# Second attention of a fused layer: order of the row maxima, two transposes of them per step, and the causal mask moved to VectorE

## The chip, the cores and the metric

One core of a Trainium2 chip (trn2) runs the whole layer in one launch. The time is that of the device for one execution, in microseconds (us); lower is better.

## The reference, cut to what matters

The layer is a first attention (16 heads of 64), a second attention (16 query heads and 4 key heads of 16, with a rotary encoding) and a mixture of 8 experts, over 4 batches of 1024 rows of 256. Only the second attention changes:

```python
# q: [4, 1024, 16, 16], k and v: [4, 1024, 4, 16] repeated for 4 query heads each
scores = jnp.einsum('bqhd,bkhd->bhqk', q, k) * scale
causal = jnp.tril(jnp.ones((S, S), dtype=bool))
scores = jnp.where(causal[None, None], scores, jnp.finfo(scores.dtype).min)
probs = jax.nn.softmax(scores, axis=-1)
attn = jnp.einsum('bhqk,bkhd->bqhd', probs, v).reshape(B, S, NH * HD)
```

## The kernel before, in words

`attention_two` goes through 16 steps, one for each batch and key head, and in each it treats four query heads. It is a software pipeline of three generations: in one step the engines prepare generation n1 (queries, keys, row maxima), compute scores, exponentials and most outputs of generation n2, and finish the last outputs of n3. The first step has only n1 and the last ones have no n1; the fourteen between run in a loop of two steps per turn. `step` of each engine is a written order over 48 slots k, one for each entry of `UNITS2`: a unit is a half c of the queries (512 columns) and a tile j of 128 keys, and it has one slot for each of the four heads. Twelve units: c=0 has j=0..3 with 512, 384, 256 and 128 columns left by the causal cut, c=1 has four of 512 and then 512, 384, 256, 128.

In each slot TensorE computes one score tile [128 keys, up to 512 queries] into one of two PSUM banks `SC` (L1252), ScalarE takes its exponential into a ring of 16 tiles `b_P` (L1175), and GpSimd cuts the diagonal ones (L1122). At the last head of a unit TensorE multiplies the four tiles of the unit two before it with the values into `b_O` (L1266); this is 8 instructions in a row.

The exponential needs the row maximum of every query first. It is subtracted inside the score product: the query operand has 96 rows of split values and two more rows, a high part `hi` and a low part `lo` of the negated maximum, against two rows of ones in the keys. The maxima come from a product of its own, [128 queries, up to 512 keys], into one of three banks `MX` (L1303), which VectorE reduces along the row (L1219). There are 48 of these a step (`MAX2`): for each head, query tile i=0..7 and key half. 32 of them hold the diagonal; there TensorE adds a mask of 128 columns with a second matmul (L1306). `FILL2` spreads the 48 over slots 4 to 38, so that some slots have two. At slot 39 VectorE takes the larger of the two halves, negates (L1225), and at slot 40 TensorE turns the 32 columns (4 heads by 8 tiles) with one transpose (L1336); VectorE makes `hi` (L1232) and `lo` (L1234), and two DMAs write them into the query operand (L1152), for the scores of the next step.

One PSUM bank, `SM`, serves four things in turn, each of which waits until the one before it has been read: the five "stacks" (slots 0, 2, 8, 17, 26: eight transposes of loaded tiles, L1293, copied by ScalarE to the keys `b_K` and the four heads' queries `b_Q`, L1184), the transpose of the maxima, and the transposes of the outputs ("turn out", slots 13 and 31, L1278), from which VectorE makes the rows `A` two slots later (L1205, L1207). SyncE loads the values and the nine pieces of the next stack, and then the two rows of the maxima, in that order in its queue.

`normalise` is the first stage of the layer and `combine` the last; the change touches only their semaphores.

Of the kernel before, what the change touches and what calls it, by code (L numbers as in the profile page):

```python
# [16 lines left out]
P = 128  # L17
# [29 lines left out]
def normalise(nc, x, hold):  # L47

    with ExitStack() as ctx:
        sb = lambda name, shape, dt=F32: ctx.enter_context(nc.sbuf_tensor(name, shape, dt))  # L50
        sem = lambda name: ctx.enter_context(nc.semaphore(name))
# [990 lines left out]
MAX2 = [(h, i, c) for h in range(GROUP) for i, c in MAXU]  # L1042
# [3 lines left out]
STACK_SLOTS = (0, 2, 8, 17, 26)  # L1046
SCORE_BANKS, MAX_BANKS = 2, 3
TURN_SLOT, OUT_SLOTS = NU2 - 8, (16 + LAG2 + 5, LAG2 + 3)
FILL2 = {k: [] for k in range(NU2)}
for _n, _k in enumerate(STACK_SLOTS):  # L1050
    FILL2[_k].append(("stack", _n))
for _n in range(NU2):
    FILL2[4 + _n * (TURN_SLOT - 5) // NU2].append(("max", _n))


def attention_two(nc, stack_dram, V2, A2):

    with ExitStack() as ctx:
# [7 lines left out]
        Q = [sb(f"b_Q{i}", [STACK + 2, GROUP, S], BF16) for i in range(2)]  # L1066
# [5 lines left out]
        minus = sb("b_minus", [P, GROUP * ST_N])  # L1072
        hi = sb("b_hi", [GROUP * ST_N, P], BF16)
        lo = sb("b_lo", [GROUP * ST_N, P], BF16)
        ident = sb("b_ident", [P, P])
        identb = sb("b_identb", [P, P], BF16)
        maskb = sb("b_maskb", [P, P], BF16)
# [7 lines left out]
                 "turn_ready", "turn_copied", "minus_in", "scores_ready", "exp_done", "masked", "pv_done",  # L1085
                 "OT_copied", "OT_ready", "inv_ready", "A2_done", "v_in", "due")
        s = {k: sem(f"b_{k}") for k in names}
        loaded = [sem(f"b_loaded{i}") for i in range(2)]
        block = ctx.enter_context(nc.Block())
# [13 lines left out]
        def _(pool):  # L1103
            for m in (ident, identb, maskb):
                pool.memset(m[:, :], 0.0).then_inc(s["consts"], 1)
# [4 lines left out]
            pool.affine_select(out=maskb[:, :], in_=maskb[:, :], compare_op=ALU.is_ge, fill=NEG, base=0,  # L1110
# [18 lines left out]
        def _(sp):  # L1129
# [8 lines left out]

            def step(n1, n2, n3, p):
                if n1 is not None:  # L1140
# [9 lines left out]
                    sp.wait_ge(s["turn_copied"], n1 * 2 + 3)  # L1150
                    for n, part in enumerate((hi, lo)):
                        sp.dma_start(Q[p][STACK + n:STACK + n + 1, :, :].rearrange("p h s -> p (h s)"), part[:, :]).then_inc(s["minus_in"], 16)  # L1152

# [4 lines left out]
        def _(act):  # L1158
# [10 lines left out]
            def step(n1, n2, n3, p):  # L1169
                for k, (c, j, h) in enumerate(UNITS2):  # L1170
# [8 lines left out]
                    if n1 is not None:  # L1179
                        for what, n in FILL2[k]:  # L1180
                            if what == "stack":
                                act.wait_ge(s["stack_ready"], n1 * (GROUP + 1) + n + 1)
# [56 lines left out]
        def _(pe):  # L1239
# [29 lines left out]
            def turn_out(n, c, turned, stacks):  # L1269
# [4 lines left out]
                if stacks is not None:  # L1274
                    pe.wait_ge(s["stack_copied"], stacks + 1)
# [686 lines left out]
```

## Time and profile before

| what | value |
|---|---|
| median of 3 runs | 3100.15 us (3084.71 to 3101.48) |
| profiled execution, its own time | 3102.33 us |
| its span, first to last instruction | 3100.0 us |
| mean granted clock of TensorE | 0.912 of full |
| second attention in it | 1664 to 2335 us |
| busy in the whole span | PE 81%, DVE 51%, ACT 48%, POOL 28% |

PE is TensorE (PEld its weight loads), DVE VectorE, ACT ScalarE, POOL GpSimd, SPq the DMA queue of SyncE. A busy matmul is shown until its modelled end, so that matmuls issued back to back overlap in the record: the issue time of one is read from the distance of two starts. "Idle before" is the time for which an engine had nothing running, and what ended it stands behind the arrow; "issue" means that nothing in the profile ended it. A line "x2" merges two instructions.

### The profile page before, as it was taken

What the parts mean: (1) busy time and instruction counts of PE and PEld (TensorE: products, weight loads), DVE (VectorE), ACT (ScalarE), POOL (GpSimd) and SP (SyncE); (2) the same over time, 40 slices, a digit from 0 to 9 for tenths busy, and PEclk for the clock granted to TensorE, in tenths of its full rate; (3) what the DMA queues carried; (4) which work ended last, traced back from release to release, by engine and by line L of the source; (5) the groups of instructions that cost most, each with busy time, mean ns of one, the idle gap of its engine ahead of it and who ended that gap; (6) DMA issues with size and microseconds to landing.
All of it is one profiled execution on the core that took longest, in us unless ns stands there. A gap on an engine that the chain in (4) does not pass through costs nothing. (4 is left out here: it accounts for less than half of the span.)

```text
span 3100.0 us, 56250 instructions
## 1 busy us (share of the span) xinstructions
PE 2526.3 (81%) x12770; PEld 1441.6 (47%) x12771; DVE 1577.3 (51%) x3757; ACT 1475.8 (48%) x3174; POOL 882.8 (28%) x1636
## 2 busy tenths in 40 slices
PE   5999998999999999999465989888886509999950
PEld 3555565555655556554332333333334505666630
DVE  6666645666366663665476666666643302222225
ACT  3555544555355553555264666666664202222212
POOL 0244423444243442445132222222221160000035
PEclk7999999999999999999787999999999559999975
DMA  2001100101000010001233011111105422111124
GB/s 96 11 25 24 38 22 17 25 24 36 17 22 24 19 36 22 17 25 29 68 127 118 17 30 30 30 30 30 30 15 180 179 97 92 46 44 46 46 63 124
DMA packets 155681, 152.47 MB, mean 49 GB/s; under 512 B 67328, under 2 KB 127744, under 8 KB 153856
## 3 DMA queue, kind: packets, MB, share of 16 engines
q1 hardware_dynamic: 139008, 124.51, 13.0%
q0 software_dynamic: 6144, 16.79, 1.6%
q10 hardware_dynamic: 10368, 9.44, 0.9%
q8 instruction: 50, 0.82, 0.1%
q14 instruction: 111, 0.91, 0.1%
HBM read 87.76 MB, written 47.45 MB: 44 GB/s over the span
## 5 line engine op out<-in xcount | busy, mean ns | idle before, releaser
L1219 DVE TENSOR_REDUCE b_peak<-b_MX 128x1 f32<-128x512 f32 (+3 forms) x768 | 379.2, 551 | 206.4 <-PE b_MX L1306 181.6
L1175 ACT ACTIVATE b_P<-b_SC 128x512 f32<-128x512 f32 (+3 forms) x768 | 350.5, 490 | 206.2 <-PE b_SC L1252 185.5
L291 POOL TENSOR_TENSOR a_A<-a_A,a_P 128x512 f32<-128x512 f32 (+3 forms) x320 | 318.0, 994 | 308.8 <-PE a_O L595 296.1
L443 ACT ACTIVATE a_P<-a_SC 128x512 f32<-128x512 f32 (+3 forms) x640 | 293.7, 469 | 234.3 <-PE a_SC L578 200.7
L501 DVE CUSTOM_DVE_ANT_0 a_MX<-a_MX,a_causal 128x128 f32<-128x128 f32 (+3 forms) x512 | 249.9, 501 | 265.4 <-PE a_MX L641 258.0
L577 PE MATMUL a_SC<-a_QR,a_KR 128*128 128x512 f32 (+3 forms) x768 | 320.1, 421 | 15.1 <-DMA a_QS<-a_minusT 11.6
L641 PE MATMUL a_MX<-a_KR,a_QR 128*128 128x512 f32 (+3 forms) x768 | 290.0, 386 | 10.4 <-DVE a_peak L501 6.2
L1122 POOL TENSOR_SCALAR_AFFINE_SELECT b_P<-b_P 128x128 f32<-128x128 f32 x512 | 147.2, 292 | 525.5 <-ACT b_P L1175 520.5
L1252 PE MATMUL b_SC<-b_Q,b_K 98*128 98x512 bf16 (+3 forms) x768 | 250.4, 339 | 33.7 <-ACT b_P L1175 31.5
L578 PE MATMUL a_SC<-a_QS,a_KS 65*128 65x512 f32 (+3 forms) x768 | 268.4, 353 | 0.0
L1722 PE MATMUL e_GU<-W,e_hT 128*128 x576 | 260.9, 596 | 1.0 <-ACT e_hT L1774 0.8
L1303 PE MATMUL b_MX<-b_K,b_Q 96*128 96x512 bf16 (+3 forms) x768 | 238.3, 340 | 17.7 <-DVE b_peak L1219 12.0
L595 PE MATMUL a_O<-a_P,a_V 128*64 128x512 f32 (+3 forms) x1280 | 234.7, 479 | 17.3 <-POOL a_P L330 14.9
L577 PEld LDWEIGHTS a_SC<-a_QR,a_KR 128*128 128x128 f32 x768 | 148.7, 194 | 183.9 <-issue 112.1
L504 DVE TENSOR_REDUCE a_peak<-a_MX 128x1 f32<-128x512 f32 x256 | 169.7, 684 | 100.1 <-PE a_MX L641 100.0
L330 POOL TENSOR_SCALAR_AFFINE_SELECT a_P<-a_P 128x128 f32<-128x128 f32 x448 | 145.7, 334 | 233.8 <-ACT a_P L443 229.5
L291 DVE TENSOR_TENSOR a_A<-a_A,a_P 128x512 f32<-128x512 f32 (+3 forms) x320 | 199.3, 623 | 22.9 <-PE a_O L595 10.2
L618 PE MATMUL a_PK<-hold,a_W 128*128 (+1 forms) x384 | 188.7, 615 | 16.2 <-DMA a_W<-in_w_pair 6.9
L1835 POOL DMA_INDIRECT c_E<-done_rows,place x64 | 70.2, 1096 | 453.9 <-PEq L1820 434.7
L1812 DVE TENSOR_TENSOR e_gate<-e_gate,e_GU 128x512 f32<-128x512 f32 x72 | 49.5, 688 | 291.4 <-PE e_GU L1722 291.4
L641 PEld LDWEIGHTS a_MX<-a_KR,a_QR 128*128 128x128 f32 x768 | 147.5, 192 | 69.5 <-DVE a_peak L501 33.5
L443 ACT ACTIVATE a_A<-a_SC 128x512 f32<-128x512 f32 x128 | 76.6, 599 | 210.0 <-PE a_SC L578 209.3
(240 smaller groups left out, 4162.3 us busy)
## 6 DMA issues: line engine op xcount, KB each, us to landing
a_inv<-inv_rows SPq DMA_DIRECT2D x128, 128.0 KB, 3.0
stack_rows<-p_stk SPq DMA_DIRECT2D x32, 480.0 KB, 2.6
a_W<-in_w_pair SPq DMA_DIRECT2D x34, 384.0 KB, 3.5
b_stk<-stack_rows SPq DMA_DIRECT2D x136, 96.0 KB, 2.0
e_G<-sorted_rows SPq DMA_DIRECT2D x74, 128.0 KB, 2.0
sorted_rows<-r_zeros SPq DMA_DIRECT2D x6, 1536.0 KB, 5.9
done_rows<-e_out ACTq DMA_DIRECT2D x72, 128.0 KB, 1.7
W<-in_w SPq DMA_DIRECT2D x8, 1024.0 KB, 11.7
```

The source lines that it names most:

```text
L291: eng.tensor_tensor(acc[h][c][:, a:], acc[h][c][:, a:], buffer(n, h)[:, a:], ALU.add).then_inc(added[h], 1)
L443: act.activation(buffer(n, h)[:, a:], SC[h][:, a:], ACT.Exp, scale=DH1 ** -0.5).then_inc(s["exp_done"], 1)
L501: dve.tensor_tensor_reduce(MX[c % MAX_BANKS1][:, 0:w], MX[c % MAX_BANKS1][:, 0:w], causal[:, BANK - w:], 1.0, 3 * NEG, ALU.add, ALU.max, p ...
L577: pe.matmul(SC[h][:, a:], KR[p][h][:, keys], QR[p][h][:, queries], start=True, stop=False)
L578: pe.matmul(SC[h][:, a:], KS[p][h][:, keys], QS[p][h][:, queries], start=False, stop=True).then_inc(s["scores_ready"], 1)
L595: pe.matmul(O[DH1 * h:DH1 * (h + 1), a:], V[p][h][:, j, :], buffer(n, h)[:, a:], start=(j == 0), stop=(n in LAST)).then_inc(s["pv_done"], 1)
L641: pe.matmul(bank[:, 0:w], QR[p][h][:, i * P:(i + 1) * P], KR[p][h][:, ch * BANK:ch * BANK + w], start=True, stop=True).then_inc(s["max_rea ...
L1175: act.activation(probs[k % RING2][:, a:], SC[k % SCORE_BANKS][:, a:], ACT.Exp, scale=DH2 ** -0.5).then_inc(s["exp_done"], 1)
L1219: dve.tensor_reduce(peak[:, h, i, ch:ch + 1], MX[n % MAX_BANKS][:, 0:w], AX.X, ALU.max).then_inc(s["max_used"], 1)
L1252: pe.matmul(SC[k % SCORE_BANKS][:, a:], K[p2][:, j * P:(j + 1) * P], Q[p2][:, h, c * BANK + a:(c + 1) * BANK], start=True, stop=True).then ...
L1303: last = pe.matmul(MX[n % MAX_BANKS][:, 0:w], Q[p][0:STACK, h, i * P:(i + 1) * P], K[p][0:STACK, ch * BANK:ch * BANK + w], start=True, sto ...
L1722: last = pe.matmul(GU[i][half][:, :], hT[i][:, kt, :], W13[:, bass.ds(e, 1), kt, half * FFN:(half + 1) * FFN].rearrange("p a f -> p (a f)" ...
```

## The change

- **Order and place of the maxima.** `MAX2` now goes by halves: first the 16 of query tiles 0 to 3 (all heads), then the 32 of tiles 4 to 7. Maximum u is placed in slot u + 5, one in every slot; the last five (43 to 47) fall into slots 0 to 4 of the next step, beside that step's first scores.
- **Two transposes.** `minus`, `hi` and `lo` exist once for each half. The first half's is turned at slot 23 of its own step, the second's at slot 6 of the next step. SyncE sends the second pair of rows at the head of its step, before the value and stack loads, and the first pair behind them. Scores of the second half wait for their rows at slot 16.
- **Stacks** at slots 0, 2, 7, 11, 15 instead of 0, 2, 8, 17, 26; the query operand is laid out by half and then head, so that ScalarE's copy writes two pieces of 512.
- **Mask.** TensorE's 32 mask matmuls are gone. VectorE reduces the 32 diagonal tiles with one instruction that adds a mask tile `causal` and takes the maximum (`tensor_tensor_reduce`, the form that the first attention uses at L501); the other 16 are reduced as before.
- **Semaphores.** `normalise`'s are kept until after `attention_two`, cleared there by GpSimd, and four of their numbers are used for `combine`'s `fetched`.

```diff
-MAX2 = [(h, i, c) for h in range(GROUP) for i, c in MAXU]
+MAX2 = [(h, i, c) for first in (True, False) for h in range(GROUP) for i, c in MAXU if (i < BANK // P) == first]
-STACK_SLOTS = (0, 2, 8, 17, 26)
+STACK_SLOTS = (0, 2, 7, 11, 15)
+MAX_START = 5
+HALF_MAX = (16, NU2)
+TURN_SLOTS = (MAX_START + 18, MAX_START + NU2 + 1 - NU2)
-TURN_SLOT, OUT_SLOTS = NU2 - 8, (16 + LAG2 + 5, LAG2 + 3)
-    FILL2[4 + _n * (TURN_SLOT - 5) // NU2].append(("max", _n))
+OUT_SLOTS = (16 + LAG2 + 5, LAG2 + 3)
+MAX_AT = {k: [n for n in range(NU2) if n + MAX_START == k] for k in range(MAX_START + NU2)}
...
 SyncE
+            def minus_rows(n, p, c):
+                sp.wait_ge(s["turn_copied"], n * 4 + 2 * c + 3)
+                for m, part in enumerate((hi[c], lo[c])):
+                    sp.dma_start(Q[p][STACK + m:STACK + m + 1, c, :, :]..., part[:, :]).then_inc(minus_in[c], 16)
+                if n2 is not None:
+                    minus_rows(n2, 1 - p, 1)
                 if n1 is not None:
...
                     load((n1 + 1) % STEPS2, 1 - p)
+                    minus_rows(n1, p, 0)
...
 VectorE
+            def reduce_max(n, u):
+                h, i, ch = MAX2[u]
+                w = min(BANK, (i + 1) * P - ch * BANK)
+                dve.wait_ge(s["max_ready"], n * NU2 + u + 1)
+                if ch == i * P // BANK:
+                    dve.sem_inc(s["due"], 1)
+                    dve.tensor_tensor_reduce(MX[u % MAX_BANKS][:, 0:w], MX[u % MAX_BANKS][:, 0:w], causal[:, BANK - w:], 1.0, 3 * NEG,
+                                             ALU.add, ALU.max, peak[:, h, i, ch:ch + 1]).then_inc(s["max_used"], 1)
+                else:
+                    dve.tensor_reduce(peak[:, h, i, ch:ch + 1], MX[u % MAX_BANKS][:, 0:w], AX.X, ALU.max).then_inc(s["max_used"], 1)
+                for c in range(2):
+                    if u == HALF_MAX[c] - 1:
+                        dve.wait_ge(s["max_used"], n * NU2 + u + 1 + MAX_BANKS)
+                        dve.tensor_reduce(minus[c][:, :, :], peak[:, :, 4 * c:4 * c + 4, :], AX.X, ALU.max,
+                                          negate=True).then_inc(s["minus_ready"], 1)
+            def turn(n, c):
+                dve.wait_ge(s["turn_ready"], n * 2 + c + 1)
+                dve.wait_ge(minus_in[c], n * 32 + 1)
+                dve.tensor_copy(hi[c][:, :], T).then_inc(s["turn_copied"], 1)
+                dve.wait_ge(s["turn_copied"], n * 4 + 2 * c + 2)
+                dve.tensor_tensor(lo[c][:, :], T, hi[c][:, :], ALU.subtract).then_inc(s["turn_copied"], 1)
...
 TensorE
-                    if diag:
-                        last = pe.matmul(MX[n % MAX_BANKS][:, w - P:w], identb[:, :], maskb[:, :], start=False, stop=True)
+                if k == 16 * c:
+                    pe.wait_ge(minus_in[c], n2 * 32 + 33)
+            def turn_minus(n, c):
+                pe.wait_ge(s["minus_ready"], n * 2 + c + 1)
+                pe.transpose(SM[0:GROUP * ST_N // 2, 0:P], ...).then_inc(s["turn_ready"], 1)
+                    if n1 is not None and k in STACK_SLOTS:
+                        n = STACK_SLOTS.index(k)
+                        if n == 0:      # loaded; rows_done(n3, 0)
...
+                        elif n == 2 and n2 is not None:
+                            turned(n2, 1)        # hi and lo of the second half read SM
+                        elif n == 4 and n3 is not None:
+                            rows_done(n3, 1)     # rows A of turn out, slot 13
+                        else:
+                            stacked(n1, n)       # ScalarE's copy before
+                        stack(n1, p, n)
+                    if n2 is not None and k == TURN_SLOTS[1]:
+                        stacked(n1, 2) ...
+                        turn_minus(n2, 1)
+                    if n1 is not None and k == TURN_SLOTS[0]:
+                        stacked(n1, 5)
+                        turn_minus(n1, 0)
...
 layer
+        nc.clear_and_free_semaphores(sems)
+        fetched = [nc.alloc_semaphore(name=f"c_fetched{i}", num=m.num) for i, m in enumerate(sems)][0:4]
```

The comments in the TensorE part of this cut are added here for the reader.

## Rows read from the trace of the kernel before

**Rows 1.** Windows over one full step: engines' busy us (instructions), granted clock, DMA.
```profile
...
2102.00:2142.70 40.70, 35.50 (x273) 15.05 (x273) 25.47 (x55) 27.12 (x56) 9.24 (x32) 1.00 0.11 29
...
```

**Rows 2.** Timeline of ScalarE: start, us, operation, idle before it.
```profile
...
1698.48 1.01 ACT L1184 ACTIVATE b_K<-b_SM 96x1024 bf16<-96x1024 bf16 x1
...
2142.24 0.60 ACT L1175 ACTIVATE b_P<-b_SC 128x512 f32<-128x512 f32 x1 [2.56 <-issue]
...
2263.28 1.01 ACT L1184 ACTIVATE b_K<-b_SM 96x1024 bf16<-96x1024 bf16 x1
...
```

**Rows 3.** Groups by shape, second attention: count, busy us, mean ns, idle before.
```profile
...
L1219 DVE TENSOR_REDUCE b_peak<-b_MX 128x1 f32<-128x512 f32 x384 | 254.7, 685 | 53.7 <-PE b_MX L1306 30.9 <-PE b_MX L1303 22.7
...
L1122 POOL TENSOR_SCALAR_AFFINE_SELECT b_P<-b_P 128x128 f32<-128x128 f32 x512 | 147.2, 292 | 525.5 <-ACT b_P L1175 520.5 <-issue 0.4
...
L1184 ACT ACTIVATE b_Q<-b_SM 96x1024 bf16<-96x1024 bf16 x64 | 65.5, 1024 | 24.9 <-PE b_SM L1293 24.8
...
```

**Rows 4.** Timeline of TensorE over one full step.
```profile
...
2100.53 0.65 PE L1293 MATMUL b_SM<-b_identb,b_stk 128*96 128x128 bf16 x8
2101.01 0.60 PE L1252 MATMUL b_SC<-b_Q,b_K 98*128 98x512 bf16 x2
...
2113.83 0.39 PE L1252 MATMUL b_SC<-b_Q,b_K 98*128 98x512 bf16 x1
...
2115.47 0.65 PE L1293 MATMUL b_SM<-b_identb,b_stk 128*96 128x128 bf16 x8 [0.91 <-DVE A L1207]
...
2135.93 0.28 PE L1336 MATMUL b_SM<-b_ident,b_minus 128*32 128x128 f32 x1 [0.26 <-DVE b_minus L1225]
...
2139.26 0.85 PE L1266 MATMUL b_O<-b_P,b_V 128*32 128x384 f32 x8
2140.05 0.64 PE L1293 MATMUL b_SM<-b_identb,b_stk 128*96 128x128 bf16 x8
...
```

**Rows 5.** Timeline of TensorE in the last step, without stacks and maxima.
```profile
...
2323.08 0.60 PE L1252 MATMUL b_SC<-b_Q,b_K 98*128 98x512 bf16 x2
2324.14 0.88 PE L1252 MATMUL b_SC<-b_Q,b_K 98*128 98x512 bf16 x2 [0.47 <-ACT b_P L1175]
2324.95 1.07 PE L1266 MATMUL b_O<-b_P,b_V 128*32 128x512 f32 x8
2325.95 0.50 PE L1252 MATMUL b_SC<-b_Q,b_K 98*128 98x384 bf16 x2
...
2328.52 0.39 PE L1252 MATMUL b_SC<-b_Q,b_K 98*128 98x256 bf16 x2
...
2330.76 0.29 PE L1252 MATMUL b_SC<-b_Q,b_K 98*128 98x128 bf16 x2
...
```

**Rows 6.** Timeline of VectorE in the step of rows 4.
```profile
...
2114.99 0.42 DVE L1207 TENSOR_TENSOR A<-b_SM,b_inv 128x256 f32 x1 [0.47 <-DVE b_inv L1205]
...
2136.68 0.28 DVE L1234 TENSOR_TENSOR b_lo<-b_SM,b_hi 32x128 bf16<-32x128 f32 x1
```

**Rows 7.** Groups by shape, VectorE in the first attention.
```profile
...
L501 DVE CUSTOM_DVE_ANT_0 a_MX<-a_MX,a_causal 128x512 f32<-128x512 f32 x128 | 88.7, 693 | 2.6
...
L501 DVE DVE_READ_ACCUMULATOR2_ANT a_peak<- 128x1 f32 x512 | 69.6, 136 | 2.7 <-issue 1.9
...
```

**Rows 8.** Timeline of VectorE in the first attention.
```profile
...
1417.46 0.69 DVE L501 CUSTOM_DVE_ANT_0 a_MX<-a_MX,a_causal 128x512 f32<-128x512 f32 x1
...
1418.07 0.33 DVE L501 CUSTOM_DVE_ANT_0 a_MX<-a_MX,a_causal 128x128 f32<-128x128 f32 x1
...
```

**Rows 9.** Timeline of TensorE from the first step into the second.
```profile
...
1694.93 1.06 PE L1293 MATMUL b_SM<-b_identb,b_stk 128*96 128x128 bf16 x8 [0.77 <-DVE b_lo L1234]
1697.35 1.04 PE L1252 MATMUL b_SC<-b_Q,b_K 98*128 98x512 bf16 x2 [1.36 <-DMA b_Q<-b_lo]
...
```

**Rows 10.** Windows of TensorE alone: busy us, granted clock.
```profile
...
1982.00:1984.00 2.00, 1.90 (x10) 0.50 0.00 0
...
2318.00:2321.00 3.00, 2.74 (x12) 0.50 0.00 0
...
```

More of the change, by code:

```diff
@@ new lines, in stacked, with turned, rows_done, stack @@
+            def stacked(n, count):
+                pe.wait_ge(s["stack_copied"], n * (GROUP + 1) + count + 1)
+            def turned(n, c):
+                pe.wait_ge(s["turn_copied"], n * 4 + 2 * c + 3)
+            def rows_done(n, c):
+                pe.wait_ge(s["A2_done"], n * 2 + c + 2)
+            def stack(n1, p, n):
+                for t in range(ST_N):
+                    last = pe.transpose(TR[:, t * P:(t + 1) * P], stk[p][:, t, (n - 1) % (GROUP + 1), :], identb[:, :])
+                last.then_inc(s["stack_ready"], 1)
@@ new lines, in maximum @@
+            def maximum(n, p, u):
+                h, i, ch = MAX2[u]
+                w = min(BANK, (i + 1) * P - ch * BANK)
+                if (i, ch) == MAXU[0]:
+                    stacked(n, h + 2)
+                pe.wait_ge(s["max_used"], n * NU2 + u + 1)
+                last = pe.matmul(MX[u % MAX_BANKS][:, 0:w], Q[p][0:STACK, i // 4, h, i % 4 * P:(i % 4 + 1) * P],
+                                 K[p][0:STACK, ch * BANK:ch * BANK + w], start=True, stop=True)
+                last.then_inc(s["max_ready"], 1)
@@ L1316, in step @@
                         output(n3, p, NU + unit)
-                    if n1 is not None:
-                        for f in FILL2[k]:
-                            fill(n1, n3, p, *f)
-                    if n2 is not None:
-                        if k == 0:
-                            scores(n2, 1 - p, 0)
-                        if last_head and unit >= 0:
-                            output(n2, 1 - p, unit)
-                        if k == OUT_SLOTS[0]:
-                            turn_out(n2, 0, n2 + 1, None if n1 is None else (n1 + 1) * (GROUP + 1))
@@ new lines, in step @@
+                    for u in MAX_AT[k]:
+                        if n1 is not None:
+                            maximum(n1, p, u)
+                    for u in MAX_AT.get(k + NU2, ()):
+                        if n2 is not None:
+                            maximum(n2, 1 - p, u)
+                    if n2 is not None and k == 0:
+                        scores(n2, 1 - p, 0)
+                    if n2 is not None and last_head and unit >= 0:
+                        output(n2, 1 - p, unit)
+                    if n2 is not None and k == TURN_SLOTS[1]:
+                        if n1 is not None:
+                            stacked(n1, 2)
+                        else:
+                            rows_done(n3, 0)
+                        turn_minus(n2, 1)
```

145 lines of the change are left out of this document (61 added, 84 removed).

## The prediction

> **What bounds the kernel now.** I read the page's slices first: the second attention lies between 1664 and 2335 us, and no engine is full in it. The chain that ended last covers only the tail of the layer, so the stage has to be read by its own rhythm. Two starts of ScalarE's key copy give the step: from 1698.48 to 2263.28 are 14 intervals, 40.34 us each [rows 2]. The windows over one step show TensorE with 35.5 busy us of 40.7, ScalarE 27.1, VectorE 25.5, GpSimd 9.2 [rows 1]; TensorE's busy time includes the modelled tails, so it is less occupied than it seems.
>
> The timeline of one step tells more [rows 4]. From stack to stack it takes 2140.05 - 2100.53 = 39.52 us; slots 0 to 15 take 13.30 of them (to 2113.83) and slots 16 to 47 take 26.22. Most other steps are about 1.1 us longer, because ScalarE comes late to its first exponential with nothing that the profile can name (2.56 us of "issue") [rows 2]. I take this as untouched by the change.
>
> The last step has no stacks and no maxima, and shows the bare rhythm of scores [rows 5]. A unit of four 512-wide tiles starts at 2323.08. Two scores are issued, 0.22 us apart (0.60 for two against 0.39 for one). The third waits for an exponential until +1.06, the output block starts at +1.87 and lasts 1.00, and the next unit starts at +2.87. So a unit is two score banks refilled at ScalarE's pace, plus what TensorE does after its last score, which ScalarE can't fill. The same rows give 2.57 for a unit of 384, 2.24 for 256 and 1.71 for 128 (2330.76, then at +0.93 an output block of 384, which takes 2140.05 - 2139.26 = 0.79 [rows 4]). Each 128 columns less in the output block save 0.21. A maximum between two scores hides in those waits; one after the fourth score does not. That is the bound: TensorE's written order, against ScalarE through two banks; VectorE comes in only where two maxima share a slot.
>
> **The change part by part.**
>
> *Slots 16 to 47.* Removed here are two stacks, the stop at slot 17 (TensorE waits 0.91 us for VectorE's rows [rows 4]), the transpose at slot 40 with its 0.26 us wait [rows 4], and the density of 1.37 maxima a slot with a mask on two of three. What is left is the bare rhythm plus one maximum after the fourth score, 0.06 to 0.22 us (0.22 for 512 columns, in proportion below). By unit: unit 4 has an output block of 256 columns, 2.87 - 0.42 + 0.17 = 2.62; unit 5 one of 128, 2.87 - 0.63 + 0.22, with the new transpose at slot 23 about 0.2, so 2.65; unit 6 3.08; unit 7 3.08 + 0.49 for turn out = 3.57 (four transposes of 128 columns, as long here as the eight of a stack, 2101.01 - 2100.53 = 0.48 [rows 4]); unit 8 3.15, as VectorE makes rows in it; units 9 to 11 2.72, 2.45 and 2.1. Sum 22.3, against 26.2: a gain of 3.9 us.
>
> *Slots 0 to 15.* Here all five stacks, one transpose of maxima and a turn out go through the one bank. I follow the order from the first stack's issue at 0, with durations from the rows. A copy takes ScalarE about 0.92 (1.02 recorded [rows 3], less the overlap of its end), and about 1.9 lie between a stack's issue and its copy's release. The second stack comes at 2.6, as now. The four new maxima put slot 4 at 4.3 (now 3.94). Slot 6 turns the second half at 5.9. The stack at slot 7 must wait until `lo` is made; from such a transpose to the end of `lo` are 2136.68 + 0.28 - 2135.93 = 1.03 us [rows 4, 6], so it starts at 7.1 and TensorE, there at 6.2, idles 0.9. Slot 8 begins at 8.1. The first maximum of the second head waits for this stack's copy until 8.9. Slot 11's stack goes at 9.7, the unit ends at 11.4. Turn out at slot 13 waits for ScalarE, which does the copy of slot 11 and then that of the outputs, until 12.1, and ends at 12.55. The stack at slot 15 has to wait for VectorE's rows: it still has the maximum of slot 14 to finish (13.3), then 1.09 for reciprocal and product (0.25, 0.42 idle-and-start, 0.42 [rows 6]), so 14.45, where TensorE has been since 12.85: 1.6 us idle against 0.9 now. Slot 16 starts at 15.9, against 13.3: a loss of 2.6 us.
>
> *Net:* -1.3 us a step, over 15 steps -19.5.
>
> *Masks.* The 32 mask matmuls are 0.06 us of issue each (a quarter of 0.22), 1.9 us a step; that gain is inside the unit prices, not beside them. VectorE takes them over. The first attention has the same instruction: 693 ns for 512 columns [rows 7] against 685 for the plain reduction [rows 3], and a read of the accumulator, 136 ns [rows 7]. The read overlaps nearly all of itself: the next instruction starts 0.61 us after the 512-wide one [rows 8]. So one costs 0.01 to 0.15 us more; I take 0.04, by the start-to-start distance, 1.3 us a step. The cover is VectorE's idle time, 15 us of 40.7 [rows 1]; above the value taken, up to 3.5 us a step would lie on VectorE, and by units it is full only in 9 to 11 (2.1 us of reductions in 2.1 to 2.7), so at most 1 us a step comes through.
>
> *First step and last.* The first loses its turn at the end: now a stack starts at 1694.93 and the first scores at 1697.35, 1.36 of it on the DMA of `lo` [rows 9]; the second step's scores will find their rows long there. That gives 2; filling only 43 maxima instead of 48 gives 2.7 on VectorE, less some 1.2 for maxima that wait for the closer stacks. The last step gains five maxima and a transpose, +1. Together -2.5.
>
> *DMAs and queues.* Each step issues four row DMAs for two, all on SyncE. The pair at the head of its step now stands before the value load and nine stack loads, whose data are needed a step later: nothing. The pair's own data take 1697.35 - 1694.9 = 2.5 us from `lo` [rows 9]; made at 7.0, they are there at 9.5, and slot 16 comes at 15.9. GpSimd's masks (292 ns each [rows 3]) don't change. Clearing the semaphores is one short work of GpSimd between two stages, taken as nothing; bound 1 us. The split copy writes as many elements: 1.02.
>
> *Sum.* The profiled execution has 3102.3 (span 3100.0); with -19.5 - 2.5 = -22 it is 3080. It lies 2 us above the median shown, so the median to come is 3078.
>
> **The rivals.**
>
> *The stalls of slots 7 and 15 cost nothing.* If ScalarE, which has three copies more in these slots, is itself the limit there, only the relief counts: -3.9 x 15 - 2.5 = -61, 3039. For it: slots 0 to 3 are ScalarE's already. Against: ScalarE has run dry by then in my walk, 0.9 us before slot 7's copy and 1.7 before slot 15's. Chance 0.15.
>
> *The one bank gets the upper hand (slower).* Seven users in 16 slots hand it on, each after the reader of the one before. If a hand-over costs 0.45 us more than walked at each of them, slots 0 to 15 take 19 us, the step is 1.8 longer, and the time is 3100 + 27 - 2.5 = 3125. It decides from 17.2 us for these slots. For it: the wait at slot 17 was 0.9 us even with four slots between turn out and stack, and VectorE may be behind. Against: VectorE has fewer maxima there. Chance 0.13.
>
> *The clock.* TensorE's clock fell to 1.2 GHz (0.50) for stretches at 1982 and 2318 [rows 10], after idle pieces at a step's head and in the thin last step. The new slots 8 to 15 have much idle time. If the clock fell there in every step, its 5 us of work would take 3 more for part of it: net +1.7 x 15, 3123. The Trainium skill ("TensorE: Matmul & The Clock Gate", Part 4: PE-mode transpose) says that the full clock does not engage for transposes, and the change crowds six groups of them into these slots; no row here parts transposes from other work, and by that rule the rival's sum would hold. Chance 0.1.
>
> *VectorE binds.* The reduction with the mask costs its full 0.15: +1 us a step, 3093. Rows 8 speak against it. Chance 0.12.
>
> **How the numbers follow.** The forecast itself has 0.5, with 3060 to 3096 as its own range (a step's net between 2.5 less and 0.1 less). About 0.5% (15 us) is what a measurement of this kernel tells from no change. Faster than 3084.6: 0.35 of my own case, 0.15 of the first rival and 0.04 of the last: 0.54. Slower than 3115.6: the second and third rival in most of their width, 0.17. Within: 0.29. Range 3040 to 3116: it takes in the first rival's value and stops short of the slow ones.
>
> **What would show it.** In the timeline of TensorE after: slot 16 some 15.9 us after the first stack of its step; waits of about 0.9 us at the stack of slot 7 for `b_lo`, and 1.6 at slot 15 for `A`; 22.3 us from there to the next stack; no wait on the DMA of the second pair; VectorE without a long idle piece between steps; the key copy every 39.0 us. The prediction is wrong if slots 0 to 15 take over 17.2 us or under 14, if half clock shows in most steps, or if the masked reductions start over 0.7 us apart.

## The result and the profile after

The changed kernel takes 3103.88 us (median of 20 runs, 3097.41 to 3117.61) against 3098.56 us for the one before (20 runs, 3084.71 to 3103.41). The ratio is 1.0025, with a 95% interval of 1.0013 to 1.0036. The forecast was 3078 us, a gain of 22. The change costs about 5 us instead: within what I called no change, but on the other side of it.

The stage can be cut out of the trace, from its first stack to the end of the last rows `A`. Before, these are 1665.18 and 2335.39, so 670.2 us; after, 1663.59 and 2336.03, so 672.4. That is 2.2 us more where 22 less were forecast. What lies outside the stage was 2429.8 us before and 2426.3 after, and goes from 2416 to 2433 over the profiled executions of this study, though nothing in it is changed. So below I give the ratio of each kernel, and the stage time of its one profiled execution. For e2 and e7 that execution lies 8 and 6 us below the median of its kernel, so their stage times are less firm than the ratios.

From the changed kernel's page, the head and the slices of the clock:

```profile
span 3098.7 us, 56383 instructions
...
PE 2511.4 (81%) x12274; PEld 1415.4 (46%) x12275; DVE 1620.2 (52%) x4317; ACT 1475.0 (48%) x3174; POOL 883.5 (29%) x1636
...
PEclk8999999999999999999786999999999559999975
```

One step of it in windows, to be set beside [rows 1]:

```profile
2141.40:2182.30 40.90, 35.48 (x242) 14.19 (x242) 28.90 (x93) 27.16 (x57) 9.28 (x32) 0.96 0.11 28
```

TensorE has 31 instructions fewer (32 masks gone, one transpose more) and is as long busy. VectorE has 3.4 us more. ScalarE and GpSimd are as before. The step is not shorter, and the granted clock is 0.96, not 1.00.

ScalarE's key copies give the mean step [rows 2]. These are the second and the last of the 16:

```profile
1693.72 1.01 ACT L1194 ACTIVATE b_K<-b_SM 96x1024 bf16<-96x1024 bf16 x1
...
2264.19 1.01 ACT L1194 ACTIVATE b_K<-b_SM 96x1024 bf16<-96x1024 bf16 x1
```

(2264.19 - 1693.72) / 14 = 40.75 us, against 40.34. The forecast had 39.0. The first copy starts at 1664.71, so first to second takes 29.01, against 32.17.

TensorE through slots 0 to 16 of one step, to be set beside the first rows of [rows 4]:

```profile
1770.60 0.65 PE L1318 MATMUL b_SM<-b_identb,b_stk 128*96 128x128 bf16 x8
...
1773.27 0.65 PE L1318 MATMUL b_SM<-b_identb,b_stk 128*96 128x128 bf16 x8 [0.51 <-ACT b_K L1194]
...
1776.86 0.28 PE L1334 MATMUL b_SM<-b_ident,b_minus 128*16 128x128 f32 x1 [0.38 <-DVE b_minus L1240]
...
1778.23 0.65 PE L1318 MATMUL b_SM<-b_identb,b_stk 128*96 128x128 bf16 x8 [0.57 <-DVE b_lo L1250]
...
1780.08 0.23 PE L1328 MATMUL b_MX<-b_K,b_Q 96*128 96x128 bf16 x1 [0.60 <-ACT b_Q L1196]
...
1780.65 0.62 PE L1318 MATMUL b_SM<-b_identb,b_stk 128*96 128x128 bf16 x8
...
1782.87 0.66 PE L1304 MATMUL b_SM<-b_ident,b_OT 128*128 128x128 f32 x4
...
1785.46 0.87 PE L1318 MATMUL b_SM<-b_identb,b_stk 128*96 128x128 bf16 x8 [1.70 <-DVE A L1222]
...
1786.58 1.51 PE L1298 MATMUL b_O<-b_P,b_V 128*32 128x384 f32 x8
...
1788.02 0.61 PE L1284 MATMUL b_SC<-b_Q,b_K 98*128 98x512 bf16 x1
```

All the stalls that I walked through are there, each a little later: the stack of slot 7 at +7.63 (forecast 7.1), slot 11's at +10.05 (9.7), slot 15's at +14.86 (14.45) after 1.70 us of waiting (1.6). Slot 16 then comes at +17.42, not at 15.9: behind the wait the output block of 384 columns takes 1.51 us where it had taken 0.85 [rows 4], because the clock has fallen. Windows of TensorE in this kernel, the first just behind that wait and the second behind the wait for `b_lo` in another step:

```profile
1786.00:1788.00 2.00, 2.00 (x13) 0.50 0.45 111
...
2148.00:2150.00 2.00, 1.97 (x11) 0.50 0.03 4
```

A step in which the clock stays full has slot 16 at +16.5.

Slots 16 to 47 of a step, TensorE again; the first row and the rows at which units 5 to 11 and the next stack start:

```profile
2157.18 0.39 PE L1284 MATMUL b_SC<-b_Q,b_K 98*128 98x512 bf16 x1
...
2159.90 0.39 PE L1284 MATMUL b_SC<-b_Q,b_K 98*128 98x512 bf16 x1
...
2162.58 0.38 PE L1284 MATMUL b_SC<-b_Q,b_K 98*128 98x512 bf16 x1
...
2165.77 0.39 PE L1284 MATMUL b_SC<-b_Q,b_K 98*128 98x512 bf16 x1
...
2169.46 0.38 PE L1284 MATMUL b_SC<-b_Q,b_K 98*128 98x512 bf16 x1
...
2172.66 0.34 PE L1284 MATMUL b_SC<-b_Q,b_K 98*128 98x384 bf16 x1
...
2175.54 0.28 PE L1284 MATMUL b_SC<-b_Q,b_K 98*128 98x256 bf16 x1
...
2178.11 0.23 PE L1284 MATMUL b_SC<-b_Q,b_K 98*128 98x128 bf16 x1
...
2179.57 0.39 PE L1328 MATMUL b_MX<-b_K,b_Q 96*128 96x512 bf16 x1 [0.24 <-DVE b_peak L1233]
...
2180.67 0.65 PE L1318 MATMUL b_SM<-b_identb,b_stk 128*96 128x128 bf16 x8
```

The units are 2.72, 2.68, 3.19, 3.69, 3.20, 2.88, 2.57 and 2.56 us: 23.49 together. The forecast had 2.62, 2.65, 3.08, 3.57, 3.15, 2.72, 2.45 and 2.1: 22.3.

The masked reductions themselves cost what was forecast. By shape:

```profile
L1236 DVE TENSOR_REDUCE b_peak<-b_MX 128x1 f32<-128x512 f32 x256 | 175.8, 687 | 5.8 <-PE b_MX L1328 5.7
...
L1233 DVE CUSTOM_DVE_ANT_0 b_MX<-b_MX,b_causal 128x512 f32<-128x512 f32 x128 | 89.7, 701 | 54.6 <-PE b_MX L1328 52.8
...
L1233 DVE DVE_READ_ACCUMULATOR2_ANT b_peak<- 128x1 f32 x512 | 72.3, 141 | 0.0
```

From the start of a 512-wide one to the next instruction it is mostly 0.61 or 0.62 us, and 0.60 for a plain one.

### The profile page after: what moved, and what is told of

Read it like the earlier page. It is cut to its first block and busy times, and to the rows that moved or that the text cites. A ratio compares the mean times of both kernels' runs of the same rounds, so it can differ in the third digit from the quotient of the medians.

```text
span 3098.7 us, 56383 instructions
## 1 busy us (share of the span) xinstructions
PE 2511.4 (81%) x12274; PEld 1415.4 (46%) x12275; DVE 1620.2 (52%) x4317; ACT 1475.0 (48%) x3174; POOL 883.5 (29%) x1636
## 3 DMA queue, kind: packets, MB, share of 16 engines
q1 hardware_dynamic: 139520, 124.52, 12.9%
q14 instruction: 144, 1.18, 0.1%
## 5 line engine op out<-in xcount | busy, mean ns | idle before, releaser
L1233 DVE CUSTOM_DVE_ANT_0 b_MX<-b_MX,b_causal 128x128 f32<-128x128 f32 (+3 forms) x512 | 251.3, 500 | 180.0 <-PE b_MX L1328 161.0
L582 PE MATMUL a_SC<-a_QR,a_KR 128*128 128x512 f32 (+3 forms) x768 | 319.7, 420 | 14.4 <-DMA a_QS<-a_minusT 11.1
L1328 PE MATMUL b_MX<-b_K,b_Q 96*128 96x512 bf16 (+3 forms) x768 | 260.1, 349 | 12.0 <-DVE b_peak L1233 5.9
L1284 PEld LDWEIGHTS b_SC<-b_Q,b_K 98*128 98x128 bf16 x768 | 74.8, 99 | 235.2 <-ACT b_P L1186 191.9
L1236 DVE TENSOR_REDUCE b_peak<-b_MX 128x1 f32<-128x512 f32 x256 | 175.8, 687 | 5.8 <-PE b_MX L1328 5.7
```

What stands on the lines that cost most here:

```text
L582: pe.matmul(SC[h][:, a:], KR[p][h][:, keys], QR[p][h][:, queries], start=True, stop=False)
L1233: dve.tensor_tensor_reduce(MX[u % MAX_BANKS][:, 0:w], MX[u % MAX_BANKS][:, 0:w], causal[:, BANK - w:], 1.0, 3 * NEG, ALU.add, ALU.max, pea ...
L1284: pe.matmul(SC[k % SCORE_BANKS][:, a:], K[p2][:, j * P:(j + 1) * P], Q[p2][:, c, h, a:], start=True, stop=True).then_inc(s["scores_ready"], 1)
L1328: last = pe.matmul(MX[u % MAX_BANKS][:, 0:w], Q[p][0:STACK, i // 4, h, i % 4 * P:(i % 4 + 1) * P], K[p][0:STACK, ch * BANK:ch * BANK + w], ...
```

## The experiments

All were timed against the kernel before, in several rounds in which its own median was 3094.5 to 3098.6 us; so kernels of different rounds are compared by their ratios, not by their medians. A step is the mean interval of the key copies; the two parts are means over the 14 steps between first and last, from the first stack to slot 16 and from there to the next stack; "full clock" is the first part in steps without half clock and without a late start of ScalarE. Half clock is summed from windows of 2 us between 1704 and 2264.

| kernel | ratio (95%) | median us | stage | step | slots 0-15 (full clock) | slots 16-47 | half clock us |
|---|---|---|---|---|---|---|---|
| before | 1 | 3098.56 | 670.2 | 40.34 | 14.40 (13.3) | 26.09 | 18 |
| after | 1.0025 (1.0013-1.0036) | 3103.88 | 672.4 | 40.75 | 17.23 (16.5) | 23.56 | 34 |
| e1 | 1.0040 (1.0026-1.0054) | 3108.62 | 684.0 | 41.14 | 14.95 (13.5) | 26.33 | 34 |
| e2 | 0.9964 (0.9949-0.9980) | 3083.29 | 657.5 | 39.82 | 16.40 (16.1) | 23.47 | 10 |
| e3 | 0.9912 (0.9894-0.9929) | 3069.30 | 635.5 | 38.22 | 14.82 (14.4) | 23.44 | 5 |
| e4 | 0.9979 (0.9968-0.9991) | 3087.13 | 666.4 | 40.27 | 16.88 (16.6) | 23.44 | 0 |
| e5 | 0.9875 (0.9854-0.9895) | 3056.13 | 632.0 | 38.04 | 14.61 (14.3) | 23.48 | 3 |
| e6 | 1.0000 (0.9985-1.0015) | 3094.82 | 668.6 | 40.38 | 14.56 (13.3) | 25.97 | 24 |
| e7 | 0.9985 (0.9972-0.9997) | 3088.10 | 660.0 | 39.54 | 14.06 (13.1) | 25.63 | 10 |
| e8 | 0.9952 (0.9934-0.9970) | 3081.21 | 658.7 | 39.94 | 16.59 (15.9) | 23.40 | 17 |
| e9 | 0.9835 (0.9823-0.9848) | 3043.13 | 618.2 | 37.21 | 14.12 (13.3) | 23.14 | 17 |
| e10 | 0.9858 (0.9841-0.9875) | 3052.27 | 628.3 | 38.03 | 14.60 (14.2) | 23.48 | 7 |
| e11 | 0.9799 (0.9787-0.9812) | 3033.82 | 611.7 | 36.73 | 13.82 (12.9) | 22.95 | 14 |

### e1: the mask alone, on the kernel before

```diff
+                                if ch == i * P // BANK:
+                                    dve.tensor_tensor_reduce(MX[...][:, 0:w], MX[...][:, 0:w], causal[:, BANK - w:], 1.0, 3 * NEG,
+                                                             ALU.add, ALU.max, peak[:, h, i, ch:ch + 1])...
-                        last = pe.matmul(MX[n % MAX_BANKS][:, w - P:w], identb[:, :], maskb[:, :], start=False, stop=True)
```

> The kernel before with one part of the change alone: the causal mask of the 32 diagonal maxima is added by VectorE and TensorE's 32 mask matmuls a step are gone; order, stacks and transposes as before. Theory of the one bank (slots 0 to 15 lose because stacks, transposes and turn out share one PSUM bank): this part brings a gain, since the maxima weigh on TensorE's order and VectorE has room: the step falls by 0.5 to 1 us, 3084 to 3091. Rival, VectorE binds: between slots 4 and 38 VectorE already does 1.37 reductions a slot, so 0.04 us more for each of 32 lengthens the step by up to 1.3 us: 3110 to 3118.

Measured: 12 us slower (0.40%), stage +13.8. So this half of the change is a loss by itself. A step at full clock is 0.5 us longer (39.5 to 40.0), and half clock is on for 34 us instead of 18. In the old order 13 of the 35 slots with maxima hold two, and TensorE waits for a bank of them. Its weight loads for the maxima, in both kernels from 1704 to 2264, show what they waited for; first before, then e1:

```profile
L1303 PEld LDWEIGHTS b_MX<-b_K,b_Q 96*128 96x128 bf16 x667 | 65.1, 98 | 77.0 <-DVE b_peak L1219 51.2 <-issue 9.1
```

```profile
L1309 PEld LDWEIGHTS b_MX<-b_K,b_Q 96*128 96x128 bf16 x658 | 63.8, 99 | 102.1 <-DVE b_peak L1222 41.9 <-DVE b_peak L1225 36.1 <-issue 7.0
```

Waits for VectorE's reduction go from 51.2 us to 78.0: every reduction longer by little, each of them in front of a waiting product.

### e2: the order alone, with the mask on TensorE

```diff
-                if ch == i * P // BANK:
-                    dve.tensor_tensor_reduce(...)
+                if ch == i * P // BANK:
+                    last = pe.matmul(MX[u % MAX_BANKS][:, w - P:w], identb[:, :], maskb[:, :], start=False, stop=True)
```

> The changed kernel with the mask back on TensorE (32 matmuls of 128 columns a step, all 48 reductions plain): the order of the maxima, the two transposes and the closer stacks alone. Theory of the one bank: the loss is in these, and the mask's matmuls come back on top: 3106 to 3116. Rival, VectorE binds: with plain reductions the units at the end of the step (slots 44 to 47, 2.55 us where 2.1 were expected) shrink to 2.1 and the time falls under that of the changed kernel, 3094 to 3100.

Measured: 3083.29 us, under both numbers. The order alone is worth 0.36%, and the mask on VectorE takes it away again. The tile `b_SM` tells where, by TensorE's waits for it. After, from 1704 to 2264:

```profile
  DVE A L1222: 23.0, 13
  DVE b_lo L1250: 7.5, 13
  ACT b_K L1194: 6.7, 13
```

and e2, from 1704 to 2200:

```profile
  DVE A L1222: 18.0, 12
  ACT b_K L1194: 6.2, 12
  DVE b_lo L1245: 2.8, 10
```

The numbers are us and times: 1.77 us each for `A` against 1.50, 0.58 for `b_lo` against 0.28. Both waits end in a chain of VectorE that starts behind its reductions, so what the masked ones cost beyond plain ones comes through there, although VectorE idles for 12 of 40.9 us. That TensorE merely arrives later in e2, since it has the mask products to do, is ruled out by e8: without any mask the wait for `A` is 1.50 us as well (18.0 us in 12 waits). VectorE's timeline shows the chain of `A`. After, three masked reductions (512, 128 and 256 columns) and the reciprocal:

```profile
2153.08 0.70 DVE L1233 CUSTOM_DVE_ANT_0 b_MX<-b_MX,b_causal 128x512 f32<-128x512 f32 x1 [0.75 <-PE b_MX L1328]
...
2154.48 0.25 DVE L1220 RECIPROCAL b_inv<-b_SM 128x16 f32<-128x16 f32 x1
```

e2, the same three as plain ones, in one row:

```profile
2130.51 1.27 DVE L1231 TENSOR_REDUCE b_peak<-b_MX 128x1 f32<-128x512 f32 x3 [0.88 <-PE b_MX L1326]
2131.70 0.25 DVE L1220 RECIPROCAL b_inv<-b_SM 128x16 f32<-128x16 f32 x1
```

That is 1.40 us before the reciprocal against 1.19; in after it is 1.40 and 1.25 in turn from step to step, in e2 always 1.19. At full clock the waits make 0.4 us a step, and half clock shrinks from 34 to 10 us as well. The unit at the end, which the rival made VectorE's, falls from 2.55 us to 2.39, not to 2.1. Slots 16 to 47 don't show it (23.47), because units 4, 9 and 10, which have the mask products back, are 0.05 to 0.07 us longer each. So the rival was right in kind and had a third of its size.

### e3: turn out behind the last stack

```diff
-OUT_SLOTS = (16 + LAG2 + 5, LAG2 + 3)
+OUT_SLOTS = (16 + LAG2 + 5, 17)
...
-                        elif n == 4 and n3 is not None:
-                            rows_done(n3, 1)
...
                     if n1 is not None and k == TURN_SLOTS[0]:
-                        stacked(n1, 5)
+                        rows_done(n3, 1)
```

> The changed kernel with one move: the transposes of the last outputs (turn out of the second half) come at slot 17, behind the last stack, instead of slot 13, so that the stack at slot 15 no longer waits for VectorE's rows A. Theory of the one bank: the 1.7 to 1.8 us of idle TensorE at slot 15 go, and most of it is kept, 1.2 to 1.8 us a step: 3077 to 3086. Rival, the clock: if the loss is TensorE's half clock in slots 7 to 17 and that comes from the idle piece at slots 6 to 7, it stays, and 3094 to 3100 remain. Rival, the wait is covered because ScalarE is the limit there: 3100 to 3106.

Measured: 3069.30, better than both. The stage falls by 36.9 us against after, from 672.4 to 635.5. Slots 0 to 15 at full clock go from 16.5 to 14.4. In the timeline of TensorE of e3 the stack of slot 15 no longer waits, and turn out fits in behind it:

```profile
2122.32 0.65 PE L1318 MATMUL b_SM<-b_identb,b_stk 128*96 128x128 bf16 x8 [0.58 <-DVE b_lo L1250]
...
2127.54 0.64 PE L1318 MATMUL b_SM<-b_identb,b_stk 128*96 128x128 bf16 x8
...
2128.28 0.85 PE L1298 MATMUL b_O<-b_P,b_V 128*32 128x384 f32 x8
...
2129.78 0.60 PE L1304 MATMUL b_SM<-b_ident,b_OT 128*128 128x128 f32 x4
```

One wait, in one of seven turns of a bank, hid the gain of the whole reordering.

### e4: the idle pieces filled with products

```diff
                         elif n == 2 and n2 is not None:
+                            again(n1, p, 2, 4)
                             turned(n2, 1)
                         elif n == 4 and n3 is not None:
+                            again(n1, p, 10, 7)
                             rows_done(n3, 1)
```

`again` repeats a product of 512 columns into a bank of the maxima that VectorE has read: 4 and 7 extra ones a step, whose results nobody reads.

> The changed kernel with repeated products in its two idle pieces: 4 extra 512-column products before TensorE's wait at slot 7 and 7 before its wait at slot 15, into the bank of a maximum that is computed again behind them, so that nothing else changes. Theory of the clock: the granted clock stays at 1.00 through the step, where it now falls to 0.50 for some 4 us in most steps (0.96 over the step), and 0.7 to 1.3 us a step come back: 3085 to 3093. Theory of the one bank alone: the clock may stay up, but the waits stand and the half clock lay beside them: 3100 to 3106.

Measured: 3087.13. Half clock is gone from all 14 steps, though TensorE does 11 products more. The step shortens by 0.48 us and the stage by 6.0. The median fell by 17, but by the two intervals that is 14 with 5 to either side, so the stage is the better price: half clock costs this kernel 6 us or somewhat more, and slots 0 to 15 keep their 16.6. The waits are the larger part.

### e5: mask on TensorE and turn out later

The edits of e2 and e3 together.

> The order and the two transposes of the change, the mask on TensorE as before, and the turn out of the second half at slot 17 behind the last stack (the two runs that were faster than the changed kernel, put together). Theory of two independent losses (the bank's chain at slot 15, and VectorE's masked reduction): they add, slots 0 to 15 fall from 16.1 to about 14.0 us, the step to 37.7 us, and the time to 3060 to 3068. Rival, both losses are one and the same wait (a masked reduction only matters because it delays VectorE's rows A): then removing the wait already got all, and this equals the run with the later turn out, 3067 to 3074, or is slower by the mask's matmuls.

Measured: 3056.13, stage 632.0. The mask's return is worth only 3.5 us of the stage once the wait for `A` is gone; 15 in the presence of that wait (672.4 to 657.5). That fits e2: most of its cost went through `A`. The medians of e3 and e5 lie 13 us apart, of which the stages explain those 3.5. The rest lies outside the stage: in the two profiled executions 2432.9 us against 2423.5, in code that is the same in both. So it is no effect of the mask, and the two intervals touch.

### e6: the same move in the old order

```diff
-TURN_SLOT, OUT_SLOTS = NU2 - 8, (16 + LAG2 + 5, LAG2 + 3)
+TURN_SLOT, OUT_SLOTS = NU2 - 8, (16 + LAG2 + 5, 19)
```

> The kernel before with one move: turn out of the second half at slot 19, behind the stack of slot 17, so that this stack doesn't wait for VectorE's rows (0.91 us there). Theory of the bank's chain: 0.5 to 0.9 us a step come back, 3083 to 3091, so that part of the gain of the later turn out has nothing to do with the change. Rival, in the order before VectorE is full between slots 4 and 38 and sets the pace: no change, 3094 to 3100.

Measured: 1.0000. Slots 0 to 15 stay at 13.3 at full clock and slots 16 to 47 are 0.1 us shorter. The rest of the 0.91 us wait of [rows 4] was covered in the old order; by what, I did not test. The same kind of wait cost 37 us of the stage in the new order.

### e7 and e8: no mask at all in the maxima

```diff
-                    if diag:
-                        last = pe.matmul(MX[n % MAX_BANKS][:, w - P:w], identb[:, :], maskb[:, :], start=False, stop=True)
```

e7 leaves the mask of the maxima out of the kernel before, e8 out of the changed one (there all reductions are plain). The mask of the exponentials stays.

> The kernel before without the causal mask in the row maxima (left out of the maxima alone; the mask of the probabilities stays): 32 matmuls of 128 columns fewer a step, all reductions plain. It prices TensorE's relief without VectorE's new cost. Theory that the masked reduction costs more than its start-to-start distance says: the relief is real, 0.5 to 1 us a step, 3083 to 3091, while moving the mask to VectorE lost 12 us. Rival, TensorE's mask matmuls were free: 3094 to 3100, and the loss of the moved mask is all VectorE's.

> The changed kernel without the causal mask in the row maxima (left out of the maxima alone): no mask matmuls and no masked reductions. It stands between the changed kernel (3104) and the run with the mask back on TensorE (3083). Theory of VectorE's masked reduction: 3075 to 3083, that is 20 us and more under the changed kernel. Rival, the clock: fewer products leave TensorE idler, half clock shows up in the steps as in the changed kernel, and the time stays at 3090 to 3100.

Measured: 0.9985 and 0.9952. So all 32 mask products together are worth 0.15% in the old order (5 us, 0.03% to 0.28%; 10 us of the one stage measured), and moving them could gain no more than that. In the new order taking the mask out altogether is hardly better than moving it back to TensorE (0.9952 against 0.9964; stages 658.7 and 657.5). But that does not make the mask products free: a step at full clock takes 39.1 us in e8 against 39.6 in e2, and half clock is on for 17 us in e8 against 10. So they cost 0.5 us a step there too, and the profiled execution gave it back in steps at half clock. The rival on record for e8 had this way of losing it, with more half clock than came; that fewer products are the reason for it was not tested by itself.

### e9: stacks respaced

On e5:

```diff
-STACK_SLOTS = (0, 2, 7, 11, 15)
+STACK_SLOTS = (0, 2, 6, 10, 14)
-MAX_START = 5
+MAX_START = 7
```

With it the second half is turned at slot 8, between the stacks of slots 6 and 10, and the first at 25, since they go by MAX_START.

> The run e5 (order and two transposes of the change, mask on TensorE, turn out at slot 17) with the users of the one bank spaced: stacks at slots 0, 2, 6, 10, 14, maxima from slot 7, so that the second half is turned at slot 8 between two stacks and each stack has five slots before the first maximum that needs its copy. Theory of the bank's chain: what is left of it, the wait for b_lo at slot 7 (0.6 us) and the wait for the copy of the second queries (0.6 us), goes; slots 0 to 15 fall by 0.5 to 1.2 us a step: 3040 to 3050. Rival, ScalarE is the limit in these slots by now (it has all five copies there): no change, 3053 to 3060.

Measured: 3043.13, in the span expected. It is the best that computes everything: 1.65% below before, 1.9% below the changed kernel. What TensorE still waits for at `b_SM` in e9, from 1704 to 2200:

```profile
  ACT b_K L1194: 6.7, 13
  DVE b_lo L1245: 2.9, 13
```

The wait for `b_lo` is 0.22 a step (0.28 in e5, 0.58 in after), and the wait for the second queries' copy, 0.5 us a step in e5, is gone like that for `A`. Slots 0 to 15 take 13.3 at full clock: what they took before, with a transpose and two stacks more in them and turn out moved behind them.

### e10: narrower reductions

On e5; the 16 plain reductions of a step read 256 of their 512 columns, so that half of these columns is left out of the maxima.

```diff
-                    dve.tensor_reduce(peak[:, h, i, ch:ch + 1], MX[u % MAX_BANKS][:, 0:w]
+                    dve.tensor_reduce(peak[:, h, i, ch:ch + 1], MX[u % MAX_BANKS][:, 0:256 if ch < i * P // BANK else w]
```

> The run e5 with less work for VectorE: the 16 reductions of the tiles off the diagonal read 256 of their 512 columns (the other half of the columns is left out of the maximum); all of them lie in slots 21 to 47 and 0 to 4, TensorE's work is the same. It asks why slots 16 to 47 take 23.5 us where 22.3 were walked. Theory that only the last unit is bound by VectorE and the rest is TensorE's signal that comes 0.12 us later when a wide maximum stands behind the score: 16 to 47 fall to 22.9 to 23.1 us, all of it in slots 44 to 47: 3044 to 3052. Rival, VectorE binds throughout: they fall to 22.3: 3034 to 3042. Rival, it binds nowhere: 23.5 stays.

Measured: 3052.27, and the step is the same: 38.03 against 38.04, slots 16 to 47 at 23.48. The theory that sent this run falls: with the mask on TensorE the reductions off the diagonal bind nowhere there, since the last unit takes 2.39 us in e5 and in e10 alike. The masked reductions are another matter. In after, e3 and e4, which have them, that unit takes 2.55 with the 0.24 us wait for `b_peak` in it, in e8, without any mask, 2.34. So they cost 0.2 us a step there.

### e11: e9 without the mask of the maxima

e9 without the 32 mask products, so the mask is left out of the maxima (the exponentials keep theirs).

> As e9, without the causal mask in the row maxima (left out of the maxima alone): neither mask matmuls nor masked reductions. It asks what the mask still costs once the bank's chain is loose. The mask's matmuls were worth 0.15% in the kernel before and nothing measurable between e2 and e8; theory: 0 to 6 us under e9. Rival, with the waits gone TensorE's order is tighter and its 1.9 us of mask matmuls a step count in full: 15 us and more under e9.

Measured: 3033.82, 0.36% below e9 by the ratios (11 us; 6.5 us of the stage). The mask products are worth 0.48 us a step here. That is what they cost at full clock in the other two orders as well (0.6 from before to e7, 0.5 from e2 to e8); from e2 to e8 half clock took it back.

## Why the prediction was wrong

**Slots 16 to 47 were mis-sized; this is the step that failed.** "Sum 22.3, against 26.2: a gain of 3.9 us." They measure 23.5 in after and in e2, e3, e4, e5 and e10 alike. The mean gain is 26.09 - 23.56 = 2.5 us. 1.4 us short in 14 steps are 20 of the 24 us between forecast and stage. The order of the terms was right, and the size of each of eight was short by 0.03 to 0.46. I took the bare rhythm from the last step and added only what follows the fourth score. In before's last step the first score starts at 2323.08 [rows 5], and its exponential at

```profile
2323.49 2.16 ACT L1175 ACTIVATE b_P<-b_SC 128x512 f32<-128x512 f32 x4 [2.38 <-PE b_SC L1252]
```

that is 0.41 us later. After, in a full step, it is 0.53; a 512-wide maximum is issued behind the score:

```profile
2165.77 0.39 PE L1284 MATMUL b_SC<-b_Q,b_K 98*128 98x512 bf16 x1
2166.00 0.38 PE L1328 MATMUL b_MX<-b_K,b_Q 96*128 96x512 bf16 x1
...
2166.30 2.27 ACT L1186 ACTIVATE b_P<-b_SC 128x512 f32<-128x512 f32 x4 [0.45 <-PE b_SC L1284]
```

The third score then starts at +1.18 (2166.95), not at +1.06. It would be natural to blame the maximum behind the score, but the first step with scores has the same maximum in the same place, and there it is 0.43:

```profile
1716.02 0.39 PE L1284 MATMUL b_SC<-b_Q,b_K 98*128 98x512 bf16 x1
1716.25 0.38 PE L1328 MATMUL b_MX<-b_K,b_Q 96*128 96x512 bf16 x1
...
1716.45 2.17 ACT L1186 ACTIVATE b_P<-b_SC 128x512 f32<-128x512 f32 x4 [0.45 <-PE b_SC L1284]
```

What parts them is the loop. Of the 16 steps with scores, the first and the last are written out, and the 14 between run in the loop. An exponential that waits for its score at full clock starts 0.10 us later inside the loop than outside it, whatever is issued behind the score, in before, after and e5 alike. In the loop the trace has a register instruction of ScalarE's sequencer for each such wait (48 a step in every run), outside none: there the value waited for is a constant. No run took the loop away, so this says where the 0.10 us lies and not by which of its parts. In after's first step with scores the eight units take 2.62, 2.58, 3.09, 3.59, 3.09, 2.88, 2.46 and 2.55: the forecast was right for units 4, 6, 7 and 10 to 0.02, and the same four are 0.10 to 0.11 longer in each step of the loop. Units 5 and 8 are 0.10 longer there too. So a maximum between two scores does hide in the waits, as the forecast had it; but the rhythm was read outside the loop and set against 26.2 us measured inside it; that is 0.6 of the 1.2 us by which the sum 22.3 is short at full clock. Before's full steps had the 0.52 as well (2129.01 to 2129.53), so it could have been read blind.

The rest is unit 11, short by 0.46, and unit 9, short by 0.16, and both were so outside the loop too. In unit 11 the masked reductions are 0.2 of it (after 2.55, e8 2.34); its scores of 128 columns and its maxima alternate without a pause to hide in. What sets the other 0.25 and unit 9 was not settled.

**Slots 0 to 15 were right in kind and by their means in size.** Forecast were 2.6 us of loss. By means it is 17.23 - 14.40 = 2.8. At full clock it is 3.2 (13.3 to 16.5), since the walk came out 0.07 us early at the second stack, 0.4 at the fifth and 0.6 at slot 16; but the late start of ScalarE, which I took as untouched, shrank. It is not without a name either: it comes in six of the 14 steps, always every second one, where the loop takes its next turn. There the trace has the branch of ScalarE's sequencer, and the first exponential starts 2.6 to 3.1 us behind it in every run (before 1814.36 to 1817.01, after 1810.86 to 1813.52). That cost did not change, but ScalarE reaches the branch earlier before the next step's first score, so that the exponential starts 0.9 to 1.0 us after that score, where it was 1.6 to 1.9. The waits came where they were forecast, at 0.57 for `b_lo` (I said 0.9, with a later arrival) and 1.7 to 1.84 for `A` (1.6). e3 shows what the second is worth with all that hangs on it: 2.5 us a step.

**The price of the mask was right, its way to the path was not.** 0.61 to 0.62 us from start to start, against 0.60, and some 0.02 to 0.07 more for each of the three in front of `A` (e2): about the 0.04 us of the forecast. But I let it lie in "VectorE's idle time, 15 us of 40.7", and charged nothing. By the full-clock steps it costs 0.4 us after (e2) and 0.5 in the old order (e1), because it stands in front of `A`, `lo` and the three banks, for which TensorE waits. It was a term at zero that cost 12 us alone (e1) and 15 us of the stage in the change (e2), net of the mask products that it saved; beside no mask at all it is 0.9 us a step at full clock (40.0 in after, 39.1 in e8). The relief of TensorE that the forecast counted is real, but 0.5 us a step and not 1.9. Slot 15's wait was computed with VectorE's time of [rows 6], without the mask's share in it. The rival of VectorE, +1 us a step, had about the size; of the place that it named, units 9 to 11, only unit 11 shows it, with 0.2.

**First and last step.** Forecast were -3.5 in the first; measured is 29.01 - 32.17 = -3.2, though it ran at half clock from 1664 to 1704. From the last key copy to the end of `A` it is 71.8 against 72.1. This holds the fifteenth full step, which is 1.3 us longer, not 1.3 shorter, and the last step. There slots 0 to 15 are 0.9 us longer, as forecast (+1), and the rest is 2.5 shorter, because before ran units 6 and 7 of it at half clock (2318 [rows 10]) and after did not. So the -0.3 agrees with the forecast's sum (-1.3 + 1) by luck.

**The clock** was a rival at 0.1, and a good part came: half clock in 10 of the 14 steps, for 34 us against 18, just behind the wait of slot 15 in three and of slot 7 in seven. e4 prices it at 0.48 us a step, not at the 1.7 net of that rival: a stretch of half clock was some 3 us long here (34 us in ten steps). My own sign for a wrong forecast, "half clock shows in most steps", is met. The Trainium skill ("TensorE: Matmul & The Clock Gate", Part 4: PE-mode transpose) says that the full clock does not engage for transposes. That they alone keep the clock down here is not so: e3 and e5 crowd nearly the same transposes into these slots and have 5 and 3 us of half clock; with 11 products in the waits and the same transposes, e4 has none. The waits at the bank are not all of it either. e9 has the shortest of them and 17 us of half clock, as before has 18, nearly all behind the idle piece at a step's head, in steps in which ScalarE starts late at the loop's turn. Transposes were not varied by themselves.

**The one bank.** This was the slower rival, "it decides from 17.2 us for these slots", and they take 17.23. The step is then no gain, as it says, but the price per hand-over is not the 0.45 it supposed: it is mostly one wait and the clock behind it. **The stalls cost nothing** falls: without the longer of the two the kernel is 35 us faster (e3), so in the changed kernel it was not ScalarE that set the pace there.

What adds up per step, from the parts: +2.8 - 2.5 = +0.3 us against 2.6 - 3.9 = -1.3, 1.6 short in 14 steps, 22 us.

## What to carry to other kernels

Where one buffer passes between several engines' short jobs, walk through each turn of it and ask which wait is not covered: move that user behind the others before judging the new order, since the same wait of 1 to 2 us cost nothing in one order and 37 us in the other. Engine idle time is no cover for work that stands in front of a hand-over; add its time to the chain that another engine waits for. And price a rhythm from a stretch inside the same loop as the one it stands for: a peeled step with the same instructions was 0.10 us a unit faster here.

## What was not expected of the hardware

- An exponential that waits for its 512-wide score starts 0.41 to 0.43 us after the start of that score in the steps outside the loop, and 0.52 to 0.53 inside it, whatever follows the score (before, after, e5). For 128 columns it is 0.27 and 0.37.
- At each turn of the loop ScalarE's first exponential comes 2.6 to 3.1 us after its branch, in all runs. In before it so starts 1.6 to 1.9 us after its score in six of 14 steps, and 0.52 after it in the others.
- TensorE's granted clock fell to 1.2 GHz (0.50) in 10 of 14 steps of after, behind waits of 0.6 us (seven times) and 1.7 us (three times) in a stretch with several short waits, for some 3 us each. Adding 11 useless products of 512 columns a step kept it at 2.4 GHz and made the kernel faster (e4 against after, 0.9979 against 1.0025).
- The masked reduction with its read of the accumulator takes 0.61 to 0.62 us from start to start at 512 columns, against 0.60 for the plain one: 141 ns of recorded read cost 10 to 20 ns of engine time.
